# A two-block network of four layers on one core: the branch for inexact ternary weights moved to the first product, the last ternary layer in whole float32, the order of steps written anew

## What is computed

```python
# 1: attention, 16 heads of 8 columns, over 1024 rows of each of 4 batches, with a layernorm of its own behind it
# 2: feed-forward with ternary weights (-1, 0, 1), _tlin(x, w, s) = (x @ w.T) * s
h = silu(_tlin(x, w1_w, w1_s)) * _tlin(x, w2_w, w2_s)      # 128 -> 512
h = gelu(_tlin(h, h1_w, h1_s), approximate=False)          # 512 -> 512
h = gelu(_tlin(h, h2_w, h2_s), approximate=False)          # 512 -> 512
return _tlin(h, w3_w, w3_s)                                # 512 -> 128
# 3: gated linear attention, 8 heads of 16 x 16, a recurrence over the rows:
h = h * exp(gt)[..., None] + kt[..., None] * vt[..., None, :];  ot = einsum('bhk,bhkv->bhv', qt, h)
# 4: a router picks 3 of 8 experts for each batch of 1024 rows; each expert is gelu(x @ Wa[e]) @ Wb[e]
```

## Time and profile before

| what | value |
|---|---|
| median of 3 runs | 1221.26 us (1220.1 to 1231.46) |
| profiled execution, its own time | 1223.53 us |
| its span in the trace | 1221.7 us |
| instructions | 16814 |

### The profile page before, as it was taken

One profiled execution on the slowest core, in us unless ns is written; L12 is line 12 of the kernel. 1 busy time (PEld: TensorE's weight loads), 2 busy tenths in 40 slices (PEclk: granted clock), 3 DMA queues, 4 the chain that ended last, 5 costly groups with the idle time before them and its releaser, 6 DMA issues.

```text
span 1221.7 us, 16814 instructions
## 1 busy us (share of the span) xinstructions
PE 1065.8 (87%) x5970; PEld 529.6 (43%) x5970; DVE 676.9 (55%) x1227; ACT 839.5 (69%) x1076; POOL 402.0 (33%) x391
## 2 busy tenths in 40 slices
PE   2899999999999999985787977887778879989998
PEld 1232333333333333324664645654544244565567
DVE  3132535343434433135447685898788989989400
ACT  2799999999998999973375555566574755624631
POOL 1000100000010100003244644677666875975300
PEclk8899999999999999996888787898887889989999
DMA  5755545354554535100000000000001001101020
GB/s 124 127 106 101 104 84 105 77 101 89 99 93 94 89 70 102 20 17 12 1 25 16 14 1 27 1 1 27 1 27 53 26 27 61 35 18 44 9 69 18
DMA packets 101456, 64.59 MB, mean 53 GB/s; under 512 B 62388, under 2 KB 91860, under 8 KB 99284
## 3 DMA queue, kind: packets, MB, share of 16 engines
q1 hardware_dynamic: 101328, 62.98, 24.8%
q10 hardware_dynamic: 24, 0.25, 0.1%
HBM read 45.10 MB, written 17.83 MB: 52 GB/s over the span
## 4 chain that ended last, share of the span: by engine, by line
PE 62%; DVE 14%; POOL 9%; ACT 7%; issue 4%; SPq 2%; DMA 2%; DVEq 0%; ACTq 0%; POOLq 0%
PE PS L1447 24%; PE PS L1432 14%; PE PS L1482 9%; PE PS L1616 5%; DVE R L1250 4%; POOL R L865 4%; PE PS L1605 3%; DVE R L1241 2%; DVE RB L1197 2%; PE PS L1376 1%; POOL R L863 1%; PE PS L1543 1%; DVE R L1203 1%; POOL RB L839 1%; DVE R L1207 1%
## 5 line engine op out<-in xcount | busy, mean ns | idle before, releaser
L902 ACT ACTIVATE R<-PS 128x1024 f32<-128x1024 f32 x512 | 474.4, 1085 | 60.2 <-PE PS L1432 59.5
L1447 PE MATMUL PS<-R 128*32 128x512 f32 x2048 | 314.6, 608 | 1.5 <-issue 1.4
L1482 PE MATMUL PS<-RB,WR 128*128 128x512 f32 x640 | 196.9, 458 | 58.3 <-DVE RB L1197 21.7
L865 POOL TENSOR_TENSOR R<-R 128x512 f32<-128x512 f32 x128 | 186.0, 1459 | 65.7 <-DVE R L1250 60.6
L1432 PE MATMUL PS<-RA 34*128 34x512 f32 x1024 | 189.3, 447 | 20.0 <-DMA RA<-QD 19.4
L1250 DVE TENSOR_TENSOR_SCAN R<-R 128x512 f32<-128x512 f32 x128 | 204.2, 1596 | 0.1
L1482 PEld LDWEIGHTS PS<-RB,WR 128*128 128x128 f32 x640 | 134.8, 215 | 110.6 <-issue 60.1
L1432 PEld LDWEIGHTS PS<-RA 34*128 34x128 f32 x1024 | 77.1, 186 | 216.8 <-issue 194.3
L922 ACT ACTIVATE R<-PS,sB 128x512 f32<-128x512 f32 x64 | 44.0, 688 | 110.3 <-PE PS L1482 109.9
L1447 PEld LDWEIGHTS PS<-R 128*32 128x32 f32 x2048 | 68.0, 108 | 106.2 <-issue 94.2
L829 POOL PARTITION_ALL_REDUCE R<-R x8 | 3.0, 376 | 289.2 <-DVE R L1089 289.2
(11 more groups left out here) (139 smaller groups left out, 1109.1 us busy)
## 6 DMA issues: line engine op xcount, KB each, us to landing
RA<-QD SPq DMA_DIRECT2D x256, 64.0 KB
QD<-RA SPq DMA_DIRECT2D x128, 64.0 KB, 2.1
RA<-QD SPq DMA_DIRECT2D x64, 128.0 KB
OD<-R SPq DMA_DIRECT2D x128, 32.0 KB, 2.0
R<-OD SPq DMA_DIRECT2D x128, 32.0 KB
VD<-R SPq DMA_DIRECT2D x24, 128.0 KB, 1.8
R<-VD SPq DMA_DIRECT2D x96, 32.0 KB
WP<-in_Wa SPq DMA_DIRECT2D x12, 256.0 KB, 2.8
```

Source lines behind the costliest of these rows:

```text
L865: pool.tensor_tensor(st, st, Qc[b % 2], ALU.mult).then_inc(S["qh"], 1)
L902: act.activation(PR[u % 4], bank(2 * s, 1024), ACT.Exp, scale=SC).then_inc(S["exp"], 1)
L1447: op = pe.matmul(bank(ob)[c:c + 32, :], VAF[b % 2][:, at:at + 32], PR[u % 4][:, 512 * h:512 * h + 512], start=(j == 0), stop=(j == 7), til ...
L1482: return pe.matmul(out_ap, l, r, **kw)
```

## The change

- `products`: the branch stands behind the first matmul of a sum, and the matmuls inside it wait for their own parts. Every later matmul of a sum is issued straight behind its own wait. The `flip` form is gone.
- `down`: no longer uses `products`. 16 plain float32 matmuls a block (4 row groups, 4 terms) from the whole values in half 1 and the weights `W3`, with no branch. It waits for the gelus (`evs[k][0]`) only.
- `gelu` of level 6 (scale 12) writes only the whole value; `level(6, ...)` has no `parts` and four steps fewer a block.
- The weights of n = 10 are not cut in two: DMA'd to `W3`, the place that `WR[:, 0, 10, :]` had. `weights` runs for n < 10; the flag comes from ten.
- `ORDER` is new: 960 letters for 992. Letters b and c fall from 115 to 99 each, all others keep their number (s 416, t 136, p 113, d 80, z 12, a 5).

```diff
-                        if key is not None:
+                        if key is not None and n < 10:
                             plan.setdefault(key, []).append(lambda bk, n=n: self.add("weights", n))
@@ level
-            self.parts(key, ("hl", dst, m), ("hl", dst, m), m % 3 == 1, None, [])
-            yield
+            if n0 == 2:
+                self.parts(key, ("hl", dst, m), ("hl", dst, m), m % 3 == 1, None, [])
+                yield
@@ build
+        W3 = WP[:, 5120:5632]
@@ sync
-                if n:
+                if 0 < n < 10:
                     need.wait_ge("w_split", n)
-                sp.dma_start(Wt, io["wB"][n]).then_inc(S["w_in"], 16)
+                sp.dma_start(Wt if n < 10 else W3, io["wB"][n]).then_inc(S["w_in"], 16)
@@ scalar
-                act.activation(HL[L][m][:, 1, :], bank(bk), ACT.Gelu, scale=sB[:, scale + m:scale + m + 1])
-                act.activation(part(HL[L][m][:, 0, :]), bank(bk), ACT.Gelu,
-                               scale=sB[:, scale + m:scale + m + 1]).then_inc(S["gelu"], 1)
+                op = act.activation(HL[L][m][:, 1, :], bank(bk), ACT.Gelu, scale=sB[:, scale + m:scale + m + 1])
+                if scale < 12:
+                    op = act.activation(part(HL[L][m][:, 0, :]), bank(bk), ACT.Gelu,
+                                        scale=sB[:, scale + m:scale + m + 1])
+                op.then_inc(S["gelu"], 1)
@@ tensor
-                for n, (i, k) in enumerate(seq[:-1]):
+                for n, (i, k) in enumerate(seq):
                     w, x, ev = terms[k]
                     need.wait_ge(*ev[i])
-                    mm(w(0), x(i), start=(n == 0), stop=False)
-                i, k = seq[-1]
-                need.wait_ge(*terms[k][2][i])
-                with pe.If_eq(ternary, 1):
-                    for i2, k2 in seq:
-                        mm(terms[k2][0](1), terms[k2][1](i2), start=False, stop=False)
-                return mm(terms[k][0](0), terms[k][1](i), start=False, stop=True)
+                    op = mm(w(0), x(i), start=(n == 0), stop=(n == len(seq) - 1))
+                    if n == 0:
+                        with pe.If_eq(ternary, 1):
+                            inner = need.inner()
+                            for i2, k2 in seq:
+                                inner.wait_ge(*terms[k2][2][i2])
+                                mm(terms[k2][0](1), terms[k2][1](i2), start=False, stop=False)
+                return op
@@ down
+                need.wait_ge("w_in", 176)
                 room(bk)
                 for i in range(4):
-                    terms = [((lambda j, k=k: WR[:, j, 10, 128 * k:128 * k + 128]),
-                              (lambda p, k=k: part(xs[k][:, p, 128 * i:128 * i + 128])), evs[k]) for k in range(4)]
-                    op = products(bank(bk)[:, 128 * i:128 * i + 128], terms, flip=True)
+                    for k in range(4):
+                        need.wait_ge(*evs[k][0])
+                        op = pe.matmul(bank(bk)[:, 128 * i:128 * i + 128], xs[k][:, 1, 128 * i:128 * i + 128],
+                                       W3[:, 128 * k:128 * k + 128], start=(k == 0), stop=(k == 3))
```

More of the change, by code:

```diff
@@ L23 @@
 ORDER = (
[L24 to L33, removed]
+    "abbbcbbccbbbaccbbcbbbbbbccbbacbbacccbbcccabccpcbbcpppbcppbppbcppppcbbppspsbscssssscscssbcbcspsscbpsb"
+    "pbssbbpspbbcpbscpcssbccsbpssbsssssscsbssspsspscbsssppscssbccspspssscsbcsbcbspsppspcpsssscsssppssbssp"
+    "bcsspbssscbsbsbstscbsspscsbptstssspsttsstcststbppssbcttcsstbcssccsbbstsbbsscttbbsscbsscscppspcpbsspb"
+    "pssppssscssssspbcssscpsptssscscssststsbsctcsstssttcsccssscsssbtssctsbssssstbtcsspbsbssppbttcstspssbp"
+    "ptbsccsspppbbspsstcstsscstbspppsspccpbpstsssssbptccsstbbsbsbcsscbtcssstbscssssbtstscttbcssscpssppcss"
+    "tsssbtsstssbccstcpssbcsstsscscstssptpsssspsssbpsscssspptssscppsssbpspsssttssttstcstbsstscssssppscszp"
+    "szsdpzstsstsdstsssdpssdstdsstssstdtppsddssstssptsdsdspdtsptpspdpptdsssstdspspssssszpstptssssdttzssss"
+    "dstssststsdtssddsstzstdtsssssssppsdpdststdssssssssdsstdsssstsspsssttttdssststsdsdstsdpstdpssppstssds"
+    "sssstspdpssdtdssststsstdssssstsststzsddszssttsssttddssstttssdsdtsststsstzsssdtssddssssstssdttsssdsss"
+    "ssdsttttdttttddttdtdtdttdtttdttzzdddzddddtdddddddddddddddddd"
 )
@@ L1152, in weights_flag @@
             def weights_flag():
-                need.wait_ge("w_split", 11)
-                dve.tensor_reduce(wmx[:, 11:12], wmx[:, 0:11], AX.X, ALU.max).then_inc(S["w_max"], 1)
+                need.wait_ge("w_split", 10)
+                dve.tensor_reduce(wmx[:, 11:12], wmx[:, 0:10], AX.X, ALU.max).then_inc(S["w_max"], 1)
                 need.wait_ge("w_max", 2)
@@ L1474, in ternary_begin, with products @@
                 pe.reg_load(ternary, flags[0:1, 8:9])
-                need.wait_ge("w_split", 11)
-            def products(out_ap, terms, flip=False):
+                need.wait_ge("w_split", 10)
+            def products(out_ap, terms):
                 def mm(w, x, **kw):
-                    l, r = (x, w) if flip else (w, x)
-                    return pe.matmul(out_ap, l, r, **kw)
+                    return pe.matmul(out_ap, w, x, **kw)
                 seq = [(i, k) for i in range(2) for k in range(len(terms))]
-                for n, (i, k) in enumerate(seq[:-1]):
+                for n, (i, k) in enumerate(seq):
                     w, x, ev = terms[k]
                     need.wait_ge(*ev[i])
-                    mm(w(0), x(i), start=(n == 0), stop=False)
-                i, k = seq[-1]
-                need.wait_ge(*terms[k][2][i])
-                with pe.If_eq(ternary, 1):
-                    for i2, k2 in seq:
-                        mm(terms[k2][0](1), terms[k2][1](i2), start=False, stop=False)
-                return mm(terms[k][0](0), terms[k][1](i), start=False, stop=True)
+                    op = mm(w(0), x(i), start=(n == 0), stop=(n == len(seq) - 1))
[6 more added lines that the diff above has]
+                return op
             def wpart(n, c0, c1):
```

## The result

The changed kernel took 1134.69 us in the median of 4 runs (1131.2 to 1137.04), the kernel before 1221.6 beside it. The ratio is 0.9274, with a 95% interval of 0.9227 to 0.932. The forecast was 1200, range 1179 to 1222: right in sign, but 87 us came off where 22 were forecast.

A forecast was written before the change was run, and what follows sets the result against it. Layer 2's chain with PE and DVE at 78% each was taken to bound 640 to 926 us, DVE at 92% the next stretch. Terms: 542 + 94 + 300 + 174 + 90 = 1200 us, range 1179 to 1222.

The forecast's parts named there:

- 94 + 300 us up to the last down: From the attention's end: 94 us (before 98) for layer 2 nearly alone, then 300 (before 286) shared with the recurrence.
- At that share 240 us take 306: Layer 2 beside the recurrence: DVE's new 240 us of load, at the old busy share, would last 306 us.
- The 0.785: Busy share of the most loaded engine before, PE's 224 of 286 us, where layer 2 and the recurrence share engines.
- A: Stretch from 640 us to the last down at 926, layer 2 beside the recurrence: 286 us before, forecast 300.
- rival 1: Moved scans fall into the holes of layer 2's chain, so its shared stretch stays at 286 us; total 1183, chance 0.26.
- The letters ahead of the first s lose only the level-6 parts: Order before the first scan: only the dropped level-6 steps go; no gain was counted for the letters.
- 224 + 15 = 239 us: PE's load where layer 2 and the recurrence share engines: 224 us before plus 15 for moved steps.
- the half of the waits: Only half counted of the downs' waits (9 us) and branches (3.6), as DVE's part is already in the load.
- the 0 for the form: Last layer's sums: plain float32 for F32R taken as worth 0, as 32 records cost 3.8 us at full clock either way.
- rival 3: Slower by the clock: granted clock falls from 0.85 to 0.79 up to the last down; 1242 us, 0.07 with Rival 4.
- Rival 4: Plain float32 costs twice F32R at 128 columns, 30 us more PE; total 1236 us, chance 0.07 together with rival 3.
- at half clock both double: Matmuls of the downs: the plain form's unmeasured half-clock price was taken to double like F32R's.

The follow-up runs named there:

- the new head: Changed kernel with only the new order's first 71 letters, all other letters in the old order's sequence: 1167.2 us, ratio 0.9523 to the kernel before.
- the first rung: Kernel before with branch first and last layer in 16 plain float32 matmuls, level 6's subtraction and the down's wait for it kept: 1210.7 us, ratio 0.9908.
- the mixed order: Changed kernel with the class of stream following the old order and the stream within each class the new: 1238.2 us, ratio 1.0109 to the kernel before.

## Why the prediction was wrong

**Right.** The attention ended at 543. The stretch behind the last down took 169 us (forecast 174) and the tail 90 (90); together 259 for 264. In the first of the two, PE was busy for 0.91 of it (0.90) and DVE for 0.93 (0.88), so DVE stayed the fuller engine, where the forecast had PE take over. A down is 32 records and takes 3.7 us at full clock, with hardly a hole. ACT loads a table 61 times for 64, the three that the list's count gave.

**Wrong: 94 + 300 us up to the last down; it took 80 + 253.** The 61 us missed are 14 ahead of the first scan and 47 behind it, and three steps of the working failed. (The forecast's cut, at 640 us, lay 7 us ahead of the first scan, so this split is good to 7 us.)

The first is "At that share 240 us take 306". The load was right, DVE had 244 us behind the first scan; but it had them in 253 us, a share of 0.97. The 0.785 was a property of the old order and code, not of the work. By my steps the order alone would have been slower (A up by 43, the next down by 34, the tail up by 2: about 1232); it was 40 us faster, and A went up by 13. That the moved scans fall into layer 2's holes stood as rival 1, and its mechanism is mostly what happened. It got 0.26, and it too took the rest of A and the 93 us ahead of it as they were: 379 for the measured 333.

The second is "The letters ahead of the first s lose only the level-6 parts". With the order alone the part ahead of the first scan fell by 16 us, and in the changed code the new head gave 19 to 20, more than half of it by five letters a, which stood visibly ahead of a gate part. The forecast had 4 us for the whole of 542 to 640, and none of them for the letters.

The third is the price of the code, in "224 + 15 = 239 us" for PE, in the half of the waits and in the 0 for the form. My steps for the code alone give 10 us (4 in the first part, 6 by A's waits, as PE's 224 stay the fuller load); it gave 38: roughly 4 for the branch, 7 for the form, 15 for the wait, 12 for the work. PE's 224 and 239 are durations of records at the clock of before, taken over as if they were work. Busy time times the granted clock of the stretch estimates the work at full clock: 295 x 0.83 = 245 us up to the last down before, and 273 x 0.92 = 251 after. At 0.83 those 251 would be 302 of busy time, so 29 us of PE's busy time came off with the clock. They are not 29 us of the 61: on the first rung the clock rose from 0.83 to 0.90, PE was busy 20 us less, and the time fell by 7 to 11. My rival 3 let the clock only fall, from the holes that an order could open; it should have asked the same of the holes that the change closes. I counted such a hole at its own length, 12.6 us for all downs, while the downs went from 47 to 30 us of busy time besides, and records behind them became shorter too.

Rival 4, a plain form twice as dear, was set aside rightly: neither form is dearer at full clock. But the conclusion "I take 0" for the form took in the sentence that at half clock both double. Both do; what I had not asked is whether the clock falls as often in both. It doesn't.

**Open.** Balance and fine order weren't separated: the run that was meant to do it told nothing, and the 55 products of the mixed order's 360 us show that letters can also lose. Each rung of the code is rough by itself. Why the clock stayed at half, or fell, in F32R matmuls of 128 columns was not tried further, nor the two forms with equal data.

## What to carry to other kernels

Read PE's busy time beside the granted clock, and turn it into work at full clock before it is called a load: a stretch with holes and a low clock has more to give than the holes' length, though less than the busy time that a higher clock takes off. In a hand-ordered list, look at which engine's queue holds a step of no hurry ahead of one that feeds PE: five letters were worth 11 to 14 us. A share of busy time measured in one order is no forecast for another; bound it by the work of the fullest engine. And where two orders are joined, look in the trace for a lump at the seam before the time is read.

## What the hardware showed beyond expectation

- Behind about 11 us of idleness, 96 F32R matmuls of 128 columns back to back stayed at 1.2 GHz for all 20.7 us, twice; 96 records of plain float32 of the same shape took 13.6 and 12.5 us and 48 F32R matmuls of 512 columns 12.7 us, all of these reaching 2.4 GHz.
- At full clock the two forms cost the same at 128 columns, 0.12 us a record, but a plain product has two records.
- Holes and form together cost more than the holes: 256 F32R records with 12.6 us of idleness among them took 47.2 us of busy time, as many plain ones with 13.6 us of it 36.4, and 33.0 and 30.0 without the holes. The granted clock fell in six of the eight F32R downs and in two of the plain ones.
